# A gated recurrence on one core: the reset gate's two products joined in the eighth step of a block too, the update gate's in steps 112 to 125, and one quarter of x ended a step later

## What is computed

```python
def step(h, inp):
    x_t, prop = inp
    comb = jnp.concatenate([x_t, h], axis=-1)
    z = jax.nn.sigmoid(comb @ Wz + bz)
    r = jax.nn.sigmoid(comb @ Wr + br)
    comb2 = jnp.concatenate([x_t, r * h], axis=-1)
    h_cand = jnp.tanh(comb2 @ Wh + bh)
    h_new = (1.0 - z) * h + z * h_cand
    h_next = jnp.where(prop, jnp.tanh(h_new @ Wp + bp), h_new)
    return (h_next, h_new)
```

## Time and profile before

| | |
|---|---|
| median of 3 runs | 1040.35 us (1040.12 to 1040.9) |
| the profiled execution | 1040.76 us |
| its span | 1038.9 us |
| PE busy | 1033.4 us (99%), 20746 matmuls |
| DVE busy | 880.9 us (85%) |
| ACT busy | 777.0 us (75%) |
| matmuls of 64 columns with `wrec_lo` or `wrec_hi` (L1360) | 13424 |
| matmuls of 128 columns (L1368) | 3248 |
| stage matmuls of 256 columns (L1274) | 3276 |

### The profile page before, as it was taken

The page is one execution under the profiler, slowest core; times in us unless marked ns, Lnnn a source line. Parts: engine busy times, 40 slices in busy tenths (PEclk is TensorE's granted clock), DMA queues, the critical chain, the costliest instruction groups (busy, mean ns, idle before and its releaser), DMA issues.

```text
span 1038.9 us, 48087 instructions
## 1 busy us (share of the span) xinstructions
PE 1033.4 (99%) x20746; PEld 953.2 (92%) x20746; DVE 880.9 (85%) x2880; ACT 777.0 (75%) x1789; POOL 0.2 (0%) x4
## 2 busy tenths in 40 slices
PE   9999999999999999999999999999999999999998
PEld 4577999999999999999999999999999999999998
DVE  6978888898989899898989989989898998876666
ACT  6877777777878778777887777878777777665565
POOL 0000000000000000000000000000000000000000
PEclk9999999999999999999999999999999999999999
DMA  9312211001111011110011110111100100000001
GB/s 331 110 43 84 84 54 44 23 23 43 43 43 43 4 44 42 44 43 23 23 44 43 44 43 11 35 44 43 44 29 17 43 23 23 23 10 17 24 24 44
DMA packets 38484, 47.26 MB, mean 45 GB/s; under 512 B 2176, under 2 KB 34048, under 8 KB 37888
## 3 DMA queue, kind: packets, MB, share of 16 engines
q1 hardware_dynamic: 38000, 44.12, 12.6%
q10 hardware_dynamic: 272, 0.07, 0.0%
HBM read 27.40 MB, written 16.78 MB: 43 GB/s over the span
## 4 chain that ended last, share of the span: by engine, by line
PE 98%; DMA 1%; SPq 0%; DVE 0%; issue 0%; ACT 0%; DVEq 0%
PE acc L1360 38%; PE x_acc L1274 34%; PE acc L1368 17%; PE x_acc L1164 8%; DMA x_part<-wz_dram 1%; PE x_acc L1295 0%; SPq L419 0%; SPq L416 0%; DVE mag_win L982 0%; SPq L425 0%; SPq L424 0%; DVE x_lo L889 0%; PE acc L1170 0%; ACT gate L745 0%; DVE new L1099 0%
## 5 line engine op out<-in xcount | busy, mean ns | idle before, releaser
L1274 PE MATMUL x_acc<-x_hi,win_hi 128*128 128x256 f16 x1092 | 298.0, 273 | 0.0
L1274 PE MATMUL x_acc<-x_lo,win_hi 128*128 128x256 f16 x1092 | 297.9, 273 | 0.0
L1274 PE MATMUL x_acc<-x_hi,win_lo 128*128 128x256 f16 x1092 | 297.9, 273 | 0.0
L589 ACT ACTIVATE gate<-gate,unscale 128x128 f32<-128x128 f32 (+1 forms) x316 | 128.6, 432 | 136.4 <-DVE gate L1067 77.7
L595 ACT ACTIVATE gate<-acc,unscale 128x128 f32<-128x128 f32 (+1 forms) x384 | 123.8, 371 | 97.9 <-PE acc L1360 97.7
L1368 PE MATMUL acc<-h_split,wrec_hi 128*128 128x128 f16 x2704 | 178.8, 220 | 0.0
L1360 PE MATMUL acc<-h_split,wrec_lo 128*128 128x64 f16 x4096 | 177.5, 194 | 0.0
L1360 PE MATMUL acc<-q_split,wrec_hi 128*128 128x64 f16 x4000 | 162.2, 194 | 0.0
L555 ACT ACTIVATE x_part<-x_acc,bias,part_unscale 128x256 f32<-128x256 f32 x312 | 154.6, 561 | 6.4 <-PE x_acc L1274 5.5
L1360 PEld LDWEIGHTS acc<-h_split,wrec_lo 128*128 128x128 f16 x4096 | 154.2, 98 | 4.7
L1368 PEld LDWEIGHTS acc<-h_split,wrec_hi 128*128 128x128 f16 x2704 | 153.7, 98 | 0.0
(11 more groups left out here) (141 smaller groups left out, 1517.5 us busy)
## 6 DMA issues: line engine op xcount, KB each, us to landing
out_dram<-x_blk SPq DMA_DIRECT2D x30, 512.0 KB, 3.2
x_blk<-x_dram SPq DMA_DIRECT2D x24, 512.0 KB, 3.8
x_blk<-x_dram SPq DMA_DIRECT2D x3, 1024.0 KB, 8.7
x_part<-wz_dram SPq DMA_DIRECT2D x4, 256.0 KB, 6.8
x_part<-wh_dram SPq DMA_DIRECT2D x4, 256.0 KB, 6.6
x_part<-wr_dram SPq DMA_DIRECT2D x1, 1024.0 KB, 10.9
x_part<-wz_dram SPq DMA_DIRECT2D x1, 1024.0 KB, 13.1
x_part<-wh_dram SPq DMA_DIRECT2D x1, 1024.0 KB, 15.3
```

What stands on the lines that cost most here:

```text
L589: nc.scalar.activation(gate[g][:, half], gate[g][:, half], func, scale=unscale[:, g:g + 1]).then_inc(gate_ready[g], 1)
L1274: mm = nc.tensor.matmul(in_halves(x_acc[bank][:])[:, j], weights[g][:, slot_w, k, j * P:(j + 1) * P], in_halves(values[m % 2][:, slot_x, : ...
```

## The change

The reset gate becomes joint in all of steps 19 to 108, which adds the eleven steps 23, 31, ... 103 (place 7 of their block). The update gate becomes joint in steps 112 to 125 as well, fourteen steps. The candidate's joint steps stay what they were. The end of stage 17 moves from place 6 to place 7, behind the end of stage 19.

```diff
@@ -33,9 +33,9 @@
 AHEAD = 32
 REC_SUM_AT = 4
 EARLY_PROP_SHARE = 1.4
-JOINT_RESET_AT = (0, 1, 2, 3, 4, 5, 6)
 AHEAD_OF_C = 4
-JOINT = range(19, 109)
+JOINT_RESET = range(19, 109)
+JOINT = (*JOINT_RESET, *range(112, 126))
 JOINT_CANDIDATE_AT = (1, 4, 6)
@@ -55,6 +55,7 @@
 STAGES_AT = [((), (0, 1)), ((), (2, 3, 4)), ((), (5, 6)), ((7, 8), (9,)), ((), (10, 11, 12)), ((), (13, 14)), ((), (15, 16, 17)), ((18, 19), (20,))]
+ENDS_AT = [(), (4,), (5,), (), (11, 12), (), (), (19, 17)]
@@ -373,15 +374,15 @@
         def behind_propagation(t):
-            return propagates(t) and joint(t) and joint(t + 1)
+            return propagates(t) and t + 1 in JOINT_RESET
         def joint_reset(t):
-            return joint(t) and t % BLOCK in JOINT_RESET_AT
+            return t in JOINT_RESET
         def joint_candidate(t):
-            return joint(t) and t % BLOCK in JOINT_CANDIDATE_AT
+            return t in JOINT_RESET and t % BLOCK in JOINT_CANDIDATE_AT
@@ -1136,8 +1137,8 @@
-                for n in stages_of(t)[0] + stages_of(t)[1]:
-                    if ORDER[n][1] in (5, 6):
+                if m + 1 in SEVEN:
+                    for n in ENDS_AT[s]:
                         end_quarter(m + 1, n)
```

## The result

| | before | after |
|---|---|---|
| median of 6 runs | 1040.7 us | 1045.98 us |
| lowest to highest | 1040.12 to 1041.55 | 1045.79 to 1046.84 |
| ratio to before, 95% interval | | 1.0052 (1.0039 to 1.0065) |
| profiled execution | 1040.76 us | 1045.79 us |
| its span | 1038.9 us | 1043.9 us |

The change costs 5.3 us by the medians and 5.0 by the two profiled executions. 5.1 was predicted.

A forecast was written before the change was run, and what follows sets the result against it. It took PE's instruction list to bound the kernel. A shorter list (-1.0 us), place 7 stalls (+4.7) and stalls in steps 112 to 125 (+1.4) gave +5.1 on the median, 1045.5 us, range 1042.9 to 1047.4.

The forecast's parts named there:

- PE's list is the time, at 29.2 and 55.6 ns: Whole kernel: PE's matmuls at these paces set the time; 25 gates made joint save 0.04 us each, 1.0 us.
- Rival 3: At all joint gates: one costs PE more than its two halves, 4.6 us over 25 gates, for 1050; chance 0.02.
- Step 59's times hold in step 63: Place 7: step 63 takes over step 59's times, so the new state comes 0.57 us later relative to PE.
- The low bound of 0.30 us per step: At stage 20, place 7: the least cost per step if only the four stage 18 matmuls moved; 3.3 us in all.
- Stage 20 waits for stage 19's end, 0.43 us in eleven steps: Place 7, steps 23 to 103: end 0.57 us later, 0.14 spare, so PE stalls 0.43 each, 4.7 in all.
- The moved end is hidden behind stage 19's: Place 7: stage 17's end delays the propagated state 0.47 us at most, covered by the stall but for 0.04.
- up to 0.3: Place 7: what the propagated state's delay would cost in us if the stall at stage 20 did not exist.
- Steps 112 to 125: 1.4 us of stalls: Joint update gate: each new state has 0.34 us less room, stalls sum to 1.4 us, net +0.8.
- the bank's 0.34: Step 125: the copy that empties the bank for a waiting matmul shifts by 0.34 us relative to PE.
- Rival 1: Place 7: stage 20 does not wait, so the kernel is not slower, 1039.3 to 1040.8 us; chance 0.10.

The follow-up runs named there:

- the fifth experiment: The whole change, but at place 7 the four matmuls of stage 18 stay behind the candidate; 1046.51 us against 1040.71 for the kernel before.
- the third experiment: The whole change, but at place 7 DVE makes stage 19's end ahead of adding the state to x; 1041.97 us against 1040.36 for the kernel before.
- fourth experiments: The whole change with the two ends at place 7 in the other order, stage 17's then stage 19's; 1053.8 us, ratio 1.0125 to the kernel before.
- The update part alone: Kernel before with only the update gate joint in steps 112 to 125, reset gate plain at place 7, stage 17's end at place 6; 1040.85 us, ratio 1.0002.
- the sixth experiment: The whole change, but the end of stage 17 stays at place 6; 1049.99 us, ratio 1.0094 to the kernel before.
- the seventh experiment: The kernel before with a joint update gate only in steps 119 to 122 and 124; 1040.48 us against 1040.71 for the kernel before.
- the first experiment: The change at place 7 only, update gate plain in steps 112 to 125 as in the kernel before; 1045.28 us against 1040.36 for that kernel.

## Why the prediction was right, point by point

- **PE's list is the time, at 29.2 and 55.6 ns.** Right, the stretches balance. From the candidate of step 19 to that of step 109 it is 712.93 us before (196.78 to 909.71) and 717.30 after (196.44 to 913.74), 4.4 more. Holes of 5.2 us after, less 0.5 of holes there before, less 11 x 0.04 for the list, make 4.2. From there to the candidate of step 126 it is 118.4 and 119.2, 0.8 more; 1.6 us of holes, less 0.3 before, less 14 x 0.04, make 0.7. Rival 3, with the 81 ns of the Trainium skill, "TensorE: Matmul & The Clock Gate", section "Back-to-back issue gap", is excluded by the new joint gates themselves: in step 63 sixteen such matmuls take 0.89 us (544.43 to 545.32 in the timeline), 55.6 ns each.
- **Step 59's times hold in step 63.** Right to the hundredth: 3.15, 3.02 and 0.57 where 3.15, 3.01 and 0.58 were taken over. But the reason given for most of the 0.57, the four matmuls ahead of the candidate, was wrong: without them the loss stays (the fifth experiment), and the cause is the reset gate's longer way over DVE. The low bound of 0.30 us per step, "only the 4 matmuls moved", stood on that reason. The number came out all the same because it was taken from step 59, where the longer way was in it.
- **Stage 20 waits for stage 19's end, 0.43 us in eleven steps.** Right in place and in what PE waits for (the third and fourth experiments), and nearly in size: 0.43 to 0.44 in nine of them. The sum was 4.7 and is 5.0, because steps 47 and 95 had 0.55 and 0.57. In the kernel before just these two already had a hole at that place, 0.21 (stage 20 at 423.88 in the earlier trace rows, where 24 matmuls from 422.97 end at 423.67) and 0.14. I had read one of the two and still gave all eleven steps the same spare. The rows of step 47, before:

```profile
421.93 0.28 DVE L1032 TENSOR_TENSOR q_split<-h_ring,q_split 128x128 f16<-128x128 f32 x1
...
422.47 0.29 DVE L1032 TENSOR_TENSOR q_split<-h_ring,q_split 128x128 f16<-128x128 f32 x1 [0.25 <-issue]
...
422.97 0.86 PE L1360 MATMUL acc<-q_split,wrec_hi 128*128 128x64 f16 x24
```

  The second half comes 0.54 after the first in place of 0.20, so 0.34 late, of which 0.14 was spare. In the change another instruction of step 47 is late, by some 0.12: the two halves of the new state take 0.61, where in step 63 they take 0.48.

```profile
422.54 0.61 DVE L1118 TENSOR_TENSOR q_split<-new,keep 128x128 f16<-128x128 f32 x2
```

  0.43 + 0.12 = 0.55. In step 95 it is a half of the candidate's operand (L1033) that comes 0.24 late; PE loses 0.10 of it at once, ahead of the matmuls on that half, and the rest ahead of stage 20, 0.43 + 0.14 = 0.57. Before, that half came 0.34 late in step 95: 0.06 at once, 0.14 ahead of stage 20, and 0.14 was spare.
- **The moved end is hidden behind stage 19's.** Right. The propagated state starts 2.36 after the propagation product (550.47 to 552.83), and before it was 2.06: 0.30 late, where I allowed 0.47, and the next reset product has no hole. The "up to 0.3" that this delay would cost without the stall's cover was 0.02 in the third experiment.
- **Steps 112 to 125: 1.4 us of stalls.** The sum was right (1.5), its parts not all. 0.06, 0.17 and 0.28 were measured as 0.05, 0.16 and 0.27, and the bank's 0.34 as 0.28. Step 119, which I took as having room, has no hole. Step 123 has 0.50 instead of 0.28. The update part alone has 0.23 there, and in the change a half of the candidate's operand is late:

```profile
1011.28 0.28 DVE L1033 TENSOR_TENSOR q_split<-q_full,q_split 128x128 f16<-128x128 f32 x1
...
1011.83 0.29 DVE L1033 TENSOR_TENSOR q_split<-q_full,q_split 128x128 f16<-128x128 f32 x1 [0.27 <-issue]
```

  It comes 0.55 after the first half in place of 0.20, so 0.35 late; PE loses 0.08 at once and the rest at the propagation product. All five kernels of these runs in which both parts stand whole (the change and the third to sixth experiments) have this hole, 0.50 each time. The timing of this part alone (0.5 us, interval -0.7 to +1.1) can't confirm the net of 0.8, only the holes can.
- **Rival 1**, that stage 20 doesn't wait, had its mechanism in the moved end of stage 17, which frees DVE at the start of place 7. It does, by 0.4 us (the sixth experiment). But this only keeps the reset sums on time, and stage 20 waits in all eleven steps.

## What to carry to other kernels

Where one engine is the bound and its list has no holes, cost a change twice: its instructions at the pace read from the starts of rows, and how much later each operand comes against the spare time at the place where the engine takes it. A shorter list here was worth 0.04 us per gate and the added way over another engine cost 0.43, so the spare time decided. Then look down the helper engine's list behind the operand that moves: the wait that bit was behind five more instructions, and the last of these, the addition of the state to x, could be put behind it at 0.02 us a step (the third experiment). Last, don't give every repeat of a step the spare time read in one: look at the place in each.

## What the runs showed of the hardware that was not expected

- DVE instructions that start late with no wait of the program, which the profile puts down to "issue", sit at fixed places of DVE's list. I took the starts of all pairs in which one DVE instruction follows another of the same line and tiles, behind 190 us, in all ten traces, and kept those over 0.06 us later than is usual for their kind: 70 rows, late by 0.11 to 0.35 us. Numbered from 0 in their trace, with DVE's semaphore waits counted, every one of them has a number that is 63 or 64 more than a multiple of 128. The delay in step 47 is number 1471 both before and in the change; there it falls on another instruction, since the list up to it is six instructions longer. The delay in step 123 is number 3647 in all five kernels that have it, and in the seventh experiment, whose list is shorter, number 3648 lies in step 124. Behind 56 of the 70 a transfer of the DMA queue that the profile calls "instruction" starts 0.57 to 0.76 us later. That points to the loading of DVE's instructions, which no run here tried. For a prediction it means that a change which adds instructions to a helper engine also moves these delays: here onto spare time, or onto a wait of PE at 0.1 to 0.3 us a time.
- PE has such places too, and there the delay differs from kernel to kernel. In step 9 of the first experiment the row reads

```profile
119.43 0.31 PE L1361 MATMUL acc<-q_split,wrec_hi 128*128 128x64 f16 x5 [0.49 <-issue]
```

  By the starts of the rows it is 0.66 us there, 0.38 in the third experiment, 0.11 before, and none over 0.02 in the change. With 0.6 us between kernels at this place alone, a difference of half a microsecond between two single profiles can't be put down to an edit before the rows show where it arises. What causes it was not tried.
- The least distance from a DVE instruction's start to the matmul that waits for it was the same in every kernel looked at: 0.80 us behind L970 (742 to 753 ns long) and 0.43 to 0.44 behind L1118 and L1055 (286 and 292 ns). From end to matmul that is 0.06 for the one and 0.15 for the others, so one latency for all would have been wrong by 0.09, a fifth of the stall.
